# All mask products and folded tap weights of the deformable stage computed by VectorE

## The reference, cut to what matters

```
x = x + deformable(_gn(x))          # 8 groups of 8 channels, 9 taps

om   = depthwise3x3(x) @ om_w.T + om_b        # 27 maps a group: 9 y offsets, 9 masks, 9 x offsets
py   = y + tap_dy + off_y ;  px = x + tap_dx + off_x
out  = sum over taps of mask * bilinear(value, py, px)
out  = out @ op_w.T
```

## Time and profile before

| | |
|---|---|
| median of three executions | 382.81 us |
| profiled execution, its own time | 380.67 us |
| its span, first to last instruction | 378.9 us |
| VectorE busy in the span | 318.3 us (84%) |
| TensorE matmul busy | 283.9 us (75%) |
| GpSimd busy | 114.3 us (30%) |
| ScalarE busy | 138.2 us (36%) |
| mean granted TensorE clock | 0.869 |

### The profile page before, as it was taken

The page is one execution under the profiler, slowest core; times in us unless marked ns, Lnnn a source line. Parts: engine busy times, 40 slices in busy tenths (PEclk is TensorE's granted clock), DMA queues, the critical chain, the costliest instruction groups (busy, mean ns, idle before and its releaser), DMA issues.

```text
span 378.9 us, 5650 instructions
## 1 busy us (share of the span) xinstructions
PE 283.9 (75%) x2078; PEld 163.2 (43%) x2078; DVE 318.3 (84%) x441; ACT 138.2 (36%) x227; POOL 114.3 (30%) x116
## 2 busy tenths in 40 slices
PE   6299486711977994649999997658988999975095
PEld 6146254500643441226766652358433433444051
DVE  6978999799836879999869796768699999998764
ACT  1034020220241586300000000068888888996000
POOL 3002299840000048999285001401380000000000
PEclk9689798955696999559999999867999999998669
DMA  4400000000000000000000000150400000000613
GB/s 130 145 18 4 7 3 2 0 0 1 2 0 2 1 0 0 0 0 2 2 2 2 2 1 2 53 156 15 142 0 0 0 0 0 2 0 3 166 55 112
DMA packets 12493, 9.73 MB, mean 26 GB/s; under 512 B 7222, under 2 KB 10806, under 8 KB 12470
## 3 DMA queue, kind: packets, MB, share of 16 engines
q1 hardware_dynamic: 10838, 8.05, 7.3%
q10 hardware_dynamic: 1632, 1.37, 1.2%
HBM read 5.23 MB, written 3.15 MB: 22 GB/s over the span
## 4 chain that ended last, share of the span: by engine, by line
PE 41%; DVE 33%; issue 16%; ACT 4%; DMA 3%; DVEq 1%; ACTq 0%
PE ps L1234 12%; PE ps L1122 11%; PE ps L1248 5%; DVE arena L361 4%; PE ps L1135 4%; DVE arena L1056 3%; DVE arena L959 3%; DVE arena L953 2%; PE ps L1327 2%; PE ps L1392 2%; PE ps L1347 1%; ACT arena L710 1%; DMA arena<-in_toep 1%; PE ps L1147 1%; DVE arena L873 1%
## 5 line engine op out<-in xcount | busy, mean ns | idle before, releaser
L1056 DVE TENSOR_TENSOR arena<-arena 128x1024 f32 x64 | 73.0, 1219 | 4.4 <-ACT arena L710 4.4
L1347 PE MATMUL ps<-arena 128*128 (+1 forms) x256 | 64.7, 380 | 6.2 <-ACT arena L710 4.9
L710 ACT ACTIVATE arena<-ps 128x2048 f32<-128x2048 f32 x32 | 60.1, 1878 | 8.5 <-PE ps L1347 7.1
L1248 PE MATMUL ps<-arena,shift 64*64 64x256 f32 x192 | 37.7, 396 | 7.9 <-DVE arena L978 7.8
L551 POOL TENSOR_TENSOR arena<-arena 128x2304 f32<-128x2304 f32 x7 | 38.4, 5501 | 13.8 <-PE ps L1248 12.7
L1347 PEld LDWEIGHTS ps<-arena 128*128 (+1 forms) x256 | 24.4, 97 | 42.1 <-issue 15.8
L1122 PE MATMUL ps<-turns,k 128*128 128x512 f32 x80 | 37.1, 626 | 6.7 <-DVE turns L943 4.9
L592 ACT ACTIVATE rstd<-mv,eps 128x2 f32<-128x2 f32 (+1 forms) x5 | 1.5, 296 | 109.8 <-DVE mv L771 109.8
L1234 PE MATMUL ps<-turns,shift 64*64 64x512 f32 x200 | 36.6, 613 | 5.8 <-DVE turns L998 5.8
L998 DVE TENSOR_TENSOR turns<-arena,ps 128x1024 f32<-128x1024 f32 x30 | 35.4, 1216 | 3.5 <-PE ps L1248 3.4
L1135 PE MATMUL ps<-arena 64*64 64x240 f32 (+3 forms) x576 | 33.5, 390 | 5.5 <-DVE arena L361 5.4
(11 more groups left out here) (221 smaller groups left out, 509.4 us busy)
## 6 DMA issues: line engine op xcount, KB each, us to landing
xs<-in_x SPq DMA_DIRECT2D x4, 256.0 KB
scratch_x<-xs SPq DMA_DIRECT2D x4, 256.0 KB
arena<-arena SPq DMA_DIRECT2D x2, 512.0 KB, 3.5
scratch_x<-arena SPq DMA_DIRECT2D x2, 512.0 KB, 3.5
arena<-scratch_x ACTq DMA_DIRECT2D x2, 512.0 KB, 3.7
out<-arena SPq DMA_DIRECT2D x4, 256.0 KB, 2.2
arena<-in_toep SPq DMA_DIRECT2D x1, 448.0 KB, 4.3
arena<-in_toep SPq DMA_DIRECT2D x1, 320.0 KB, 3.0
```

Of the source, the lines that this page charges most:

```text
L710: act.activation(E[k], ps[:, (k % 2) * 2048:(k % 2 + 1) * 2048], ACT.Exp, scale=0.5 / SPLIT ** 2, accum_out=rowsum[:, bass.ds(i, 1)]).then ...
L1056: dve.tensor_tensor(out=cc, in0=cc, in1=E[k][:, lo * P:hi * P], op=ALU.add).then_inc(sem(name), 1)
L1248: return pe.matmul(slot(s, 64 * j, 64), view(w, 64 * i, [(1, 64)], 64 * i, 64), view(folds[f % len(folds)], col * PX, [(1, PX)], 64 * i, 6 ...
L1347: ins = pe.matmul(bank(b0 + q), w, m[:, bass.ds(i * P + 512 * q, 512)], start=(t == 0), stop=(t == 1 and q > 0))
```

## The change

Everything that GpSimd did between clearing the border of `vpad` (L520) and clearing `colacc` (L555) is taken away: two mask products and eight folds. VectorE issues all of them, with the same shapes and operands. Mask products 0 and 1 stand behind each other before the transposes of the third portion of maps, mask product 2 behind the hats of the first six horizontal maps, fold 0 behind it. Folds 1 and 2 stand directly before the first window product, folds 3 to 5 before slot 5's, 6 and 7 before slot 10's, 8 before slot 15's. Waits for `over`, `maps_done` and the last horizontal maps, which GpSimd had in front of folds 3 to 5, now stand on VectorE in front of folds 1 and 2. TensorE's and ScalarE's lists are unchanged.

```diff
--- before.py
+++ after.py
@@ -518,39 +518,6 @@
 
             pool.wait_ge(sem("x1_ready"), 8)
             pool.memset(view(vpad, 0, [(320, 8), (288, 2), (1, 2 * HW)]), 0.0).then_inc(sem("vpad_zero"), 1)
-
-            def mask_hats(dy):
-
-                v = view(hy, dy * 3 * PX, [(W, 3), (1, 3 * PX)])
-                pool.tensor_tensor(out=v, in0=v, in1=view(omX, W + dy * 3 * PX, [(0, 3), (1, 3 * PX)]),
-                                   op=ALU.mult).then_inc(sem("masked_late"), 1)
-
-            pool.wait_ge(sem("maps_turned"), 8)
-            pool.wait_ge(sem("hats_y"), 2)
-            pool.wait_ge(sem("middle_y"), 2)
-            mask_hats(1)
-            pool.wait_ge(sem("maps_turned"), 12)
-            mask_hats(2)
-            for i in range(1, len(FOLDS)):
-                by, dy = FOLDS[i]
-                if i == 1:
-                    pool.wait_ge(sem("masked_first"), 1)
-                    pool.wait_ge(sem("masked_late"), 2)
-                    pool.wait_ge(sem("hats_x"), 1)
-                    pool.wait_ge(sem("middle_x"), 1)
-                if i == 3:
-                    pool.wait_ge(sem("over"), 1)
-                if i == 4:
-                    pool.wait_ge(sem("maps_done"), 16)
-                    pool.wait_ge(sem("maps_turned"), 16)
-                if i == 5:
-                    pool.wait_ge(sem("hats_x"), 2)
-                    pool.wait_ge(sem("middle_x"), 2)
-                if i >= len(folds):
-                    pool.wait_ge(sem("slot_ready"), ROW * (FOLDS[i - len(folds)][0] + 1))
-                pool.tensor_tensor(out=view(folds[i % len(folds)], 0, [(3 * PX, 3), (PX, 3), (1, PX)]),
-                                   in0=view(hy, (by - dy) * W + dy * 3 * PX, [(PX, 3), (0, 3), (1, PX)]),
-                                   in1=view(hx, dy * 3 * PX, [(PX, 3), (W, 3), (1, PX)]), op=ALU.mult).then_inc(sem("folded"), 1)
             pool.wait_ge(sem("window_done"), 1)
             pool.memset(colacc[:, 0:REACH * P], 0.0).then_inc(sem("col_near"), 1)
             pool.memset(colacc[:, REACH * P:48 * P], 0.0).then_inc(sem("col_far"), 1)
@@ -965,25 +932,50 @@
             turn_maps(1)
             dve.wait_ge(sem("maps_turned"), 8)
             hats(hy, offy, 8, 1, "hats_y")
-            dve.wait_ge(sem("hats_y"), 1)
+
+            def mask_hats(dy):
+
+                v = view(hy, dy * 3 * PX, [(W, 3), (1, 3 * PX)])
+                dve.tensor_tensor(out=v, in0=v, in1=view(omX, W + dy * 3 * PX, [(0, 3), (1, 3 * PX)]),
+                                  op=ALU.mult).then_inc(sem("masked"), 1)
+
+            def fold(i, name):
+
+                by, dy = FOLDS[i]
+                if i >= len(folds):
+                    dve.wait_ge(sem("slot_ready"), ROW * (FOLDS[i - len(folds)][0] + 1))
+                dve.tensor_tensor(out=view(folds[i % len(folds)], 0, [(3 * PX, 3), (PX, 3), (1, PX)]),
+                                  in0=view(hy, (by - dy) * W + dy * 3 * PX, [(PX, 3), (0, 3), (1, PX)]),
+                                  in1=view(hx, dy * 3 * PX, [(PX, 3), (W, 3), (1, PX)]), op=ALU.mult).then_inc(sem(name), 1)
+
+            dve.wait_ge(sem("hats_y"), 2)
             dve.wait_ge(sem("middle_y"), 1)
-            v = view(hy, 0, [(W, 3), (1, 3 * PX)])
-            dve.tensor_tensor(out=v, in0=v, in1=view(omX, W, [(0, 3), (1, 3 * PX)]), op=ALU.mult).then_inc(sem("masked_first"), 1)
+            mask_hats(0)
+            dve.wait_ge(sem("middle_y"), 2)
+            mask_hats(1)
             turn_maps(2)
             dve.wait_ge(sem("maps_turned"), 12)
             hats(hx, offx, 0, 6, "hats_x")
-            dve.wait_ge(sem("masked_first"), 1)
+            dve.wait_ge(sem("masked"), 2)
+            mask_hats(2)
             dve.wait_ge(sem("hats_x"), 1)
             dve.wait_ge(sem("middle_x"), 1)
-            dve.tensor_tensor(out=view(folds[0], 0, [(3 * PX, 3), (PX, 3), (1, PX)]),
-                              in0=view(hy, 0, [(PX, 3), (0, 3), (1, PX)]),
-                              in1=view(hx, 0, [(PX, 3), (W, 3), (1, PX)]), op=ALU.mult).then_inc(sem("fold_first"), 1)
+            fold(0, "fold_first")
             turn_maps(3)
             dve.wait_ge(sem("maps_turned"), 16)
             hats(hx, offx, 6, 3, "hats_x")
 
             for p in range(SLOTS):
                 by, bx = divmod(p, ROW)
+                if p == 0:
+                    dve.wait_ge(sem("masked"), 3)
+                    dve.wait_ge(sem("over"), 1)
+                    dve.wait_ge(sem("maps_done"), 16)
+                    dve.wait_ge(sem("hats_x"), 2)
+                    dve.wait_ge(sem("middle_x"), 2)
+                if bx == 0 and by + 1 < ROW:
+                    for i in range(folded_by[by] + 1, folded_by[by + 1] + 1):
+                        fold(i, "folded")
                 if p == 20:
                     dve.wait_ge(sem("over"), 2)
                     dve.tensor_reduce(oversum, over[:, 0:2], AX.X, ALU.add).then_inc(sem("over_rows"), 1)
```

## The result

The changed kernel took 391.60 us (median of four executions, 390.71 to 392.29) against 382.85 for the kernel before (four, 381.44 to 383.19). The ratio is 1.0234, 95% interval 1.0200 to 1.0268: slower by 8.8 us. The forecast was 390.3, range 385.8 to 396.3. The profiled execution took 390.71 us with a span of 388.6, so 9.7 us more span than before.

What follows compares the result with a forecast made beforehand. The prediction took TensorE to bound the window, with small slack on VectorE. Lead-in -1.3, window folds +7.9 and TensorE's clock +0.9 gave +7.5 us on the median 382.81: 390.3, 8-in-10 range 385.8 to 396.3.

Steps and rivals of the forecast that it cites:

- lead-in: Before the first window product: quiet hats save 12.2 us, mask products and folds add 4.9 each, a wait 0.95; taken as -1.3.
- row 1 with the clock's fall: Second window row: three folds on VectorE add 6.2 us, TensorE's slower clock after the pause at slot 5 adds 0.9.
- The hats' stretch was a lock on GpSimd: Before the window: four VectorE hats waited for whole GpSimd instructions; free of GpSimd they take 2.6 us, saving 12.2.
- Part of the folds falls into VectorE's slack: In the window: of 14.8 us of folds moved to VectorE, 6.9 fall into time it waited before, leaving +7.9.
- The clock falls once, at slot 5: At slot 5 TensorE idles 5.5 us, then runs 2.75 us at half speed: +0.9 us, bounds 0 and 1.4.
- The later pauses: TensorE idles 3.3 us at slot 10 and 0.8 at slot 15, nothing counted; clock falls at every pause would add 1.8.
- The sign set for the waits: In the window: VectorE's waits for slot building were to go from 7.5 us to under 2.5.
- Everything behind the window moves as one: After the window: all later work, GpSimd's clearing of `colacc` included, shifts together, with no term of its own.
- Nothing is absorbed: Rival, chance 0.14: in the window TensorE loses as much per pause as VectorE; all folds count, +13.5 us, 396.3.
- More is absorbed: Rival, chance 0.11: no clock fall, the lead-in gains 2.4 us and all idle times fill; +3.8 us, 386.6.
- Not slower: Rival, chance 0.04: all 50 window products get faster with GpSimd quiet, mean at or under 1.07 us; 382.8.
- The hats are slow for another reason: Rival, chance 0.03: before the window the hats stay at 14.8 us despite quiet GpSimd; +19.7 us, 402.5.

Runs made afterwards that it cites:

- the run with idle work: The changed kernel plus 22 small unused matmuls on TensorE behind slot 4's second addition, filling its pause at slot 5: 388.83 us, ratio 1.0169.

## Why the prediction was right, step by step

| step | predicted | measured |
|---|---|---|
| lead-in | -1.3 | -1.2 (27.7 to 26.5) |
| row 0 | 0 | +0.6 (12.2 to 12.8) |
| row 1 with the clock's fall | +7.1 | +7.6 (12.7 to 20.3) |
| row 2 | +1.6 | +1.6 (15.4 to 17.0) |
| row 3 | +0.1 | +0.7 (13.8 to 14.5) |
| row 4 and the step behind it | 0 | 0 (14.2 to 14.2) |
| behind the window | 0 | +0.6 |
| ahead of the lead-in | 0 | -0.2 |
| sum | +7.5 | +9.7 |

- *The hats' stretch was a lock on GpSimd.* Right, and shown by adding GpSimd work and nothing else that takes time. The 12.2 us saved by quiet hats were 12.0: the two stretches of four hats, 14.76 us before, took 2.8 us (1.74 and 1.03) and not 2.6, the 0.2 that the prediction had allowed for a fixed part of each instruction.
- *Mask products and folds at a pitch of 2.47 us, a wait of 0.95 before fold 1.* Right: two at 5.03, and 0.91. But to take the wait away is worth nothing: without it the window gave back 0.8 of the 1.0 us.
- *Part of the folds falls into VectorE's slack.* Right in kind: of 14.8 us, 10.5 stayed, clock included, where I had 8.8.
- *The clock falls once, at slot 5.* Right, after 5.44 us of idle TensorE where I had 5.5. The size was off. I took 2.75 us at half clock from one instance; here it was 4.4, and in row 0, where I expected no change, 3.9 us:

```profile
164.56:168.50 3.94, 3.94 (x23) 2.13 (x27) 3.25 (x3) 0.00 (x0) 0.00 (x0) 0.50 0.00 0
```

  TensorE started 1.4 us earlier than in the kernel before and the clock rose at nearly the same moment, so row 0 grew by 0.6 (the wait for slot 2 is 1.09 us and not 0.51), and slot 5's pause cost 1.5 (by the run with idle work) and not 0.9. These are the two terms that were too small.
- *The later pauses.* The prediction expected TensorE to idle 3.3 us at slot 10. It idled 0.83: it had more left to do there than the reckoning gave it. Since nothing was counted for it, the sum did not suffer. The clock stayed at 1.00 in rows 2 and 3, so the case in which every pause makes it fall did not come.
- *Rows 2 and 3.* Row 2 came as forecast, its wait of 0.66 us at slot 13 included. In row 3 two waits of 0.26 and 0.23 us for slot building remained, where I let none remain.
- *The sign set for the waits.* Missed: VectorE's waits for slot building were to fall under 2.5 us and fell to 3.9, of which 2.7 are the waits behind the two stretches at half clock (1.09, 0.23, 1.19 and 0.23).
- *Everything behind the window moves as one.* Wrong by 0.6 us. The clock fell behind the window in this trace and not in the one before; the product there grew by 1.7 us, the transposes after it shrank by 1.1.
- *Rivals.* "Nothing is absorbed" would have needed +13.5. "More is absorbed" needed a clock that does not fall. "Not slower" needed faster window products, and they stayed at 1.21 us with GpSimd quiet. "The hats are slow for another reason" is out, since they ran in 0.96 and 0.56 us.

Little of this was luck: the errors of the terms do not cancel, nearly all of them lie on the slow side, and together they make the 2.2 us by which the profile passed the forecast.

What stays open: at which moment the clock falls and rises. With the same work behind the window, that product took 7.1 us in the profiles of five kernels and 8.8 in those of seven.

## What to carry to other kernels

When an instruction takes several times what its columns ask for, look at what GpSimd does in the same microseconds, and move the two apart before moving work from one to the other: keeping them apart gave -4.8 us where moving everything cost +8.8. In these traces VectorE work with one input in PSUM (1.21 us) and its transposes (four in 3.70 us beside a fold, 3.69 with GpSimd quiet; 3.83 beside mask products, 3.73 quiet) lay beside GpSimd at next to no cost; the one-input float32 hats (up to 5.80 us in place of 0.95) and products of two SBUF tiles (7.39 in place of 2.55) did not. Work put on an engine that only waits a little is free at most up to that wait, and here it was cheaper in single pieces between the steps of the loop, by 3.3 us, than in blocks that let the engine behind it fall idle. Set one by one, the six folds of 14.8 us made the window 7.4 us longer, while VectorE's waits for slot building fell from 7.5 to 1.1 us.

## What the runs showed of the hardware

- GpSimd instructions that only write block VectorE's one-input float32 SBUF hats as well: 3.88 and 4.77 us in place of 0.96 and 0.95.
- A VectorE product of two SBUF tiles waited 4.9 us for a GpSimd product begun 0.08 us earlier (7.39 in place of 2.55).
- TensorE's work at half clock after a pause was 2.75, 3.9 and 4.4 us in three cases with pauses of 5.8, 5.8 and 5.4 us; in the first two the clock was at half before the pause too. With folds 0 to 2 on VectorE the same pause of 5.76 us as in the changed kernel was followed by 4.5 us at half clock and not 3.9. It is not one price.
- Unused matmuls in the pauses held the granted clock at 1.00. In the kernel before no gain shows in the total (382.04 us, ratio 0.9989); in the kernel with GpSimd kept apart they went with 3.0 us (377.81 to 374.79).
